# A state-space layer with a gated projection stage on one core: opening rebuilt, last stage's first chunk by pairs

## The reference

```
h   = layernorm(layernorm(x)) * gamma + beta
xz  = h @ W_in.T                          # 512 -> 2048: x_ssm and z, 1024 channels each
xs  = silu(conv4(x_ssm) + conv_b)         # causal, per channel
xp  = xs @ W_xproj.T                      # 33 columns: 1, B (16), C (16)
dt  = softplus(xp @ W_dt.T + b_dt) + 0.001
A   = -exp(A_log)                         # 1024 x 16
h_t = clip(dA*h + (1-dA)/(A+1e-8)*B_t*xs_t, -10, 10),  dA = exp(A*dt_t)
y_t = sum_n C_t[n]*h_t[n] + D*xs_t
x   = x + (y * silu(z)) @ W_out.T
u   = layernorm(x)
x   = x + u @ W_shared.T + bias + (sum of the two normalized top gate weights) * (u @ W_expert.T)
```

## Time and profile before

| | us |
|---|---|
| Median of three runs | 4454.98 (4453.03 to 4458.05) |
| Profiled execution | 4454.84 |
| Its span | 4453.1 |
| PE busy | 4166.3 (94%) |
| DVE busy | 3676.1 (83%) |
| ACT busy | 3171.4 (71%) |
| POOL busy | 3138.2 (70%) |

### The profile page before, as it was taken

The page is one execution under the profiler, slowest core; times in us unless marked ns, Lnnn a source line. Parts: engine busy times, 40 slices in busy tenths (PEclk is TensorE's granted clock), DMA queues, the critical chain, the costliest instruction groups (busy, mean ns, idle before and its releaser), DMA issues. The chain is left out here.

```text
span 4453.1 us, 48998 instructions
## 1 busy us (share of the span) xinstructions
PE 4166.3 (94%) x14186; PEld 2461.5 (55%) x14186; DVE 3676.1 (83%) x4321; ACT 3171.4 (71%) x5821; POOL 3138.2 (70%) x1550
## 2 busy tenths in 40 slices
PE   2999999995999999999999999999999759999999
PEld 1777777774444444444444444444444238888887
DVE  5888888884899999999999999999999744444443
ACT  1666666664899999999999999999999611211111
POOL 0111111110899999999999999999999767777772
PEclk9999999997999999999999999999999879999999
DMA  5566566666576576656665766576656445555550
GB/s 187 190 203 207 186 208 212 214 205 196 152 191 189 155 184 185 184 155 186 187 181 156 193 186 172 158 197 188 168 168 181 142 157 162 169 163 175 176 166 30
DMA packets 581176, 786.71 MB, mean 177 GB/s; under 512 B 102800, under 2 KB 305936, under 8 KB 579368
## 3 DMA queue, kind: packets, MB, share of 16 engines
q1 hardware_dynamic: 570344, 762.57, 58.4%
q10 hardware_dynamic: 10560, 20.97, 1.3%
HBM read 540.17 MB, written 245.18 MB: 176 GB/s over the span
## 5 line engine op out<-in xcount | busy, mean ns | idle before, releaser
L965 POOL TENSOR_TENSOR q<-g,cc 128x1024 f32<-128x1024 f32 x1024 | 2394.6, 2371 | 139.7 <-DVE g L1105 120.6
L1105 DVE TENSOR_TENSOR_SCAN g<-dd,carry,ps_a 128x512 f32<-128x512 f32 x2048 | 2400.3, 1253 | 40.2 <-ACT ps_a L987 24.5
L1045 PE MATMUL ps_y<-q,w_s 128*128 128x512 f32 x4096 | 2098.4, 593 | 24.4 <-POOL q L965 12.7
L987 ACT ACTIVATE ps_a<-dt_s,small 128x512 f32<-128x512 f32 x2048 | 1501.7, 733 | 5.4 <-DVE g L1105 5.4
L976 ACT ACTIVATE dd<-ps_d 128x512 f32<-128x512 f32 x2048 | 1287.7, 629 | 74.7 <-PE ps_d L1032 51.7
L1032 PE MATMUL ps_d<-dm,xk 99*128 99x512 f32 x2048 | 1119.1, 547 | 63.7 <-ACT dd L976 25.9
L1032 PEld LDWEIGHTS ps_d<-dm,xk 99*128 99x128 f32 x2048 | 384.0, 188 | 1223.0 <-ACT dd L976 957.7
L1045 PEld LDWEIGHTS ps_y<-q,w_s 128*128 128x128 f32 x4096 | 778.6, 191 | 184.7 <-issue 59.3
L353 POOL TENSOR_TENSOR xnt_lo<-xnt_f,xnt_hi 128x512 fp32r<-128x512 f32 x64 | 112.5, 1758 | 557.1 <-ACT xnt_hi L378 557.1
L499 PE MATMUL ps_r_f<-xnt_hi,w_hi 128*128 128x512 f32 x1024 | 418.5, 409 | 13.8 <-DVE w_lo L672 13.8
L499 PE MATMUL ps_r_f<-xnt_lo,w_hi 128*128 128x512 f32 x1024 | 402.9, 393 | 0.0
(11 more groups left out here) (162 smaller groups left out, 4439.5 us busy)
## 6 DMA issues: line engine op xcount, KB each, us to landing
w_s<-w_d SPq DMA_DIRECT2D x256, 512.0 KB, 3.8
xk<-xt_d SPq DMA_DIRECT2D x768, 132.0 KB
xt_d<-xt_f SPq DMA_DIRECT2D x256, 256.0 KB, 3.1
cc<-c_d SPq DMA_DIRECT2D x128, 512.0 KB, 11.3
dm<-band_d SPq DMA_DIRECT2D x192, 264.0 KB
xs_d<-xs_f SPq DMA_DIRECT2D x128, 256.0 KB, 2.5
zs_d<-zs_f SPq DMA_DIRECT2D x128, 256.0 KB, 3.0
dt_d<-lg_f SPq DMA_DIRECT2D x32, 1024.0 KB, 6.5
```

The costliest lines, as they stand in the source:

```text
L965: pool.tensor_tensor(q[:, s % QB:s % QB + 2, :], g[:, s % GB:s % GB + 2, :], rows, ALU.mult).then_inc(s_q, 2)
L987: act.activation(ps_a[:, s % AB, :], dt[:, blk % DTB, :], ACT.Exp, scale=small[:, blk % MD, S_A + n:S_A + n + 1]).then_inc(s_a, 1)
L1045: pe.matmul(ps_y[:, blk % 2, :], w[:, half % WB, at:at + P], q[:, s % QB, :], start=(n == 0), stop=(n == NS - 1)).then_inc(s_n, 1)
L1105: dve.tensor_tensor_scan(g[:, s % GB, :], dd[:, m % 2, n, :], ps_a[:, s % AB, :], carry[:, m, n:n + 1], ALU.add, ALU.mult).then_inc(s_g, 1)
```

## The change

- `setup` is gone. Its POOL memsets and DVE steps move into `front`'s streams; the DVE steps stand behind the lowering of the weights, in smaller tiles that share room with the convolution buffers. `small` stays in SBUF for both stages, without D.
- W_in comes in four transfers of 1 MB (a semaphore each) and is copied and lowered by quarters between the scalings of x. PE's first projection waits for each quarter. x of chunk 1 is loaded before the edges are cleared and before `w_dt` is repaired.
- The diagonals are no longer computed: SP writes zeros to `w_d` (two transfers of 0.5 MB in each of chunks 0 to 7) and then the 2048 diagonal elements of one m (in chunks 1 to 8). The band is cleared in chunks 8 to 11, from a smaller tile of zeros. The transposed inverse goes by way of PE and one DVE copy in chunk 0 to `invt_d`, three times and once as zeros.
- `fill_band(0)` moves to chunk 12 of the front, `gather_ahead` to its end; both must land before the front ends.
- In `ffn` SP issues all loads. Chunk 0 comes by pairs of groups (xs, y and zs of a pair count on one semaphore); some of it waits in `y_lo`, `t_hi`, `t_lo`. Its split runs by pairs, and PE projects the lower half of the channels between the last four row products. The inverse takes four groups of 16 rows, so b and c rows come in two transfers instead of six.

```diff
+                load_x(0)
+                for dst, src in ((a_log, ...), (gamma[:, :], t_in["ln_gamma"]), (beta[:, :], t_in["ln_beta"])):
+                    sp.dma_start(dst, src).then_inc(s_gb, 16)
+                for k in range(KD):
+                    sp.dma_start(raw_win[k], t_in["W_inT"][k * P:(k + 1) * P, :]).then_inc(s_wq[k], 16)
...
+                load_x(1)
+                sp.wait_ge(s_pool, 1)
+                clear_edges()
+                sp.wait_ge(s_lo, KD + 1)
                 sp.dma_start(w_dt[2 * NX:NX3, :].bitcast(F32), low_dt.bitcast(F32)).then_inc(s_wt, 16)
-                load_x(1)
...
+                def clear_diagonal(m, h):
+                    sp.dma_start(w_d[m, :, bass.ts(h, NS * P // 2)].rearrange("p (n k) -> p n k", k=P),
+                                 bcast(zeros[:, 0:1], [(0, NS // 2), (1, P)])).then_inc(s_zero, 16)
+                def fill_diagonal(m):
+                    whole = w_d[m, :, :]
+                    sp.dma_start(bass.AP(tensor=whole.tensor, offset=whole.offset, ap=[(W_PITCH + 1, P), (P, NS)]), inv[:, m, :],
+                                 allow_slow_non_contiguous=True).then_inc(s_diag, 16)
...
                     store_b(ch)
+                    if 0 < ch <= MD:
+                        sp.wait_ge(s_zero, 16 * (EDGES + 2 * ch))
+                        fill_diagonal(ch - 1)
+                    if ch < MD:
+                        clear_diagonal(ch, 0)
+                    elif ch < MD + 4:
+                        clear_band(ch - MD)
+                    elif ch == MD + 4:
+                        sp.wait_ge(s_bto, 32)
+                        sp.wait_ge(s_zero, 16 * (EDGES + 2 * MD + 8))
+                        fill_first_band()
                     store_zs(ch, 6)
                     store_turned(ch, 6)
                     load_x(ch + 2)
                     store_zs(ch, 7)
                     store_turned(ch, 7)
+                    if ch < MD:
+                        clear_diagonal(ch, 1)
...
                 sp.wait_ge(s_xpo, CHUNKS * 32)
+                for b in range(BATCH):
+                    gather_ahead(b)
+                sp.wait_ge(s_diag, 16 * (4 + MD + 2 + BATCH))
...
+                act.wait_ge(s_gb, 48)
+                act.activation(ea, a_log, ACT.Exp).then_inc(s_ea, 1)
+                upper_win(0)
+                scale_xnt(0, 0)
+                scale_xnt(0, 1)
+                upper_win(1)
+                scale_xnt(0, 2)
+                scale_xnt(0, 3)
+                upper_win(2)
+                upper_win(3)
+                act.wait_ge(s_wt, 9 * 16)
                 act.activation(w_dt[:, :], raw_dt, ACT.Copy).then_inc(s_hi, 1)
...
-                fill_band(0)
-                sp.dma_start(small[:, :, :], w_d[:, :, W_BIG:W_COLS].rearrange("m p s -> p m s"), ...)
                 load_x(0, 0)
-                sp.wait_ge(s_band, 32)
                 load_b(0, 0)
...
                 load_c(0, 3)
-                for b in range(BATCH):
-                    gather_ahead(b)
-                sp.wait_ge(s_ba, 16 * BATCH)
                 load_ahead(0)
...
+                load_rows(0)
+                sp.dma_start(raw_inv, invt_d).then_inc(s_wt[0], 16)
                 sp.dma_start(d_par[:, :], t_in["D_param"]).then_inc(s_dp, 16)
-                load_first(0)
-                load_y(0)
+                load_pair(0)
+                load_pair(1)
+                load_weights(1, "W_outT", 0)
+                load_pair(2)
+                load_pair(3)
+                load_weights(2, "W_outT", HALF * P)
                 load_x(0)
+                load_weights(4, "W_expertT", 0)
+                sp.wait_ge(s_hi, 1)
+                sp.wait_ge(s_lo, 1)
+                load_weights(3, "W_sharedT", 0)
...
-                for m in range(MD):
+                pe.wait_ge(s_set, 4)
+                for m in range(HALF):
                     weigh(0, m)
+                for i in range(SUB):
+                    weigh(0, HALF + i)
+                    if i == 0:
+                        pe.wait_ge(s_lo, 2)
+                    project(0, i, 0)
                 pe.wait_ge(s_lo, 3)
                 for i in range(SUB):
-                    project(0, i, 0)
                     project(0, i, 1)
                     weigh(1, 2 * i)
                     weigh(1, 2 * i + 1)
```

More of the change, by code:

```diff
@@ L176, in front @@
-def front(nc, sb, sem, t_in, ident, ones, minus_half, margin, within, clips, xs_d, dt_d, zs_d, xp_d, xt_d, bt_d, c_d):
+            front(nc, sb, sem, t_in, ident, ones, minus_half, margin, within, clips, small, xs_d, dt_d, zs_d, xp_d, xt_d, bt_d, c_d,
+                  band_d, w_d, invt_d, ba_d)
+        scan(nc, sb, sem, clips, small, xs_d, dt_d, xt_d, bt_d, band_d, c_d, w_d, y_d, ba_d)
+        ffn(nc, sb, sem, t_in, ident, minus_half, xs_d, zs_d, xp_d, invt_d, y_d, out)
+def front(nc, sb, sem, t_in, ident, ones, minus_half, margin, within, clips, small, xs_d, dt_d, zs_d, xp_d, xt_d, bt_d, c_d,
+          band_d, w_d, invt_d, ba_d):
@@ L217, in front @@
         S = lambda n: sem("f_" + n, c)
-        s_wt, s_x, s_one, s_hi, s_lo, s_b1 = S("weights"), S("x"), S("one"), S("hi"), S("lo"), S("b1")
+        s_wt, s_x, s_one, s_hi, s_lo = S("weights"), S("x"), S("one"), S("hi"), S("lo")
+        s_wq = [S(f"wq{k}") for k in range(KD)]
+        s_gb, s_pool, s_ea, s_set = S("gb"), S("pool"), S("ea"), S("set")
+        s_ivm, s_ivt, s_zero, s_diag = S("ivm"), S("ivt"), S("zero"), S("diag")
         s_st, s_pow, s_xn, s_tr, s_te, s_xl = S("stats"), S("pow"), S("xn"), S("tr"), S("te"), S("xl")
@@ L229, in front, with plain @@
         raw_dt = xs[0:NX3, 0:2, :].rearrange("p m t -> p (m t)")
+        raw_win = [t[:, h * XHALF:(h + 1) * XHALF, :].rearrange("p m t -> p (m t)") for t in (v, lg) for h in range(2)]
+        a_log, ea, ap_, an = (conv[:, 1, bass.ts(i, MD * NS)].rearrange("p (m n) -> p m n", n=NS) for i in range(4))
+        raw_invt = v[0:NS, 0:2, :].rearrange("p m t -> p (m t)")
         low_dt = xt[0:NX, 0, 0:2, :].rearrange("p s t -> p (s t)")
+        def plain(ch, q):
+            return conv[:, 0, :] if ch == 0 and q % 2 else xnt[:, :]
         def made(ch, kind, m):
@@ L310, in _ @@
                     store_xs(ch, 3)
+                    if ch == 0:
+                        sp.wait_ge(s_ivt, 1)
+                        for r in range(3):
+                            sp.dma_start(invt_d[NS * r:NS * (r + 1), :, :].rearrange("n m p -> n (m p)"), raw_invt).then_inc(s_diag, 16)
+                        sp.dma_start(invt_d[3 * NS:4 * NS, :, :], bcast(zeros[0:NS, 0:1], [(0, MD), (1, P)])).then_inc(s_diag, 16)
                     store_zs(ch, 0)
@@ L742, in _, with scan @@
                 dve.wait_ge(s_fl, 3)
-def scan(nc, sb, sem, ident, clips, xs_d, dt_d, xp_d, xt_d, bt_d, band_d, c_d, w_d, y_d, ba_d):
+def scan(nc, sb, sem, clips, small, xs_d, dt_d, xt_d, bt_d, band_d, c_d, w_d, y_d, ba_d):
     STEPS = MD * NS
@@ L778, in scan @@
         S = lambda n: sem("s_" + n, c)
-        s_sm, s_band, s_ba = S("small"), S("band"), S("ba")
+        s_band, s_ba = S("band"), S("ba")
         s_dm = [S(f"dm{i}") for i in range(PIECES)]
@@ L1360, in upper_weights, with upper_first @@
                     act.activation(parts[i][1], parts[i][0], ACT.Copy).then_inc(s_hi, 1)
-                def upper_inverse():
-                    act.wait_ge(s_wt[0], 96)
-                    for h in range(2):
-                        last = act.activation(inv[:, h::2, :], raw_inv[h], ACT.Copy)
-                    last.then_inc(s_hi, 1)
+                def upper_first(j):
+                    act.wait_ge(s_mul, 2 * j + 2)
+                    act.activation(y_hi[:, 2 * j:2 * j + 2, :], y[:, 2 * j:2 * j + 2, :], ACT.Copy).then_inc(s_yh, 1)
                 def upper_y(ch):
```

362 lines of the change are left out of this document (159 added, 203 removed).

## The result

| | before | after |
|---|---|---|
| Median (6 runs each) | 4453.09 us (4451.33 to 4458.05) | 4472.84 us (4455.33 to 4474.16) |
| Ratio, 95% interval | | 1.0033 (1.0023 to 1.0043) |
| Profiled execution, span | 4454.84, 4453.1 us | 4471.99, 4470.2 us |
| Granted clock over the span | 0.981 | 0.976 |

Slower, by 0.3% (0.2 to 0.4; the medians alone differ by 0.44%); the forecast was 4360 us, 2% faster than before. Five of the six runs of after lie between 4471.2 and 4474.2, one at 4455.33; that one has no trace, so it stays unexplained.

A forecast was written before the change was run, and what follows sets the result against it. It took PE to bound front chunks and POOL's products to pace the scan, with gains only where they wait. -64.6 + 8 - 2.2 + 3 - 11 - 28 = -94.8 on 4453.1 gave 4358.3, predicted 4360 us; 4343 to 4375 at 0.65.

The forecast's parts named there:

- A: Opening: without `setup`, x loads first and weights come by quarters; gain 64.6 us, bounds 60 and 66.
- B: Front chunks: added zero and diagonal transfers on SP delay the load of x; loss 8 us, bounds 0 and 16.
- slack of 2.2 us: Front chunk: what DVE can lose to late x, 1.1 after the statistics and 1.1 at the turned tile.
- sign of being wrong: Front chunks: the prediction is wrong if a chunk period, expected at 59.7 us, grows by over 2.
- The forecast of 8: Front chunks: loss taken from an overflow of 13.6 us, less because chunks where x has margin give less.
- x is late by more than costed: Rival, front: SP's issues of thousands of descriptors also hold up stores; loss 20 to 40 us, chance 0.13.
- C: Into the scan: dropped band fill and `small` load gain 2.2 us; the gather at front's end loses 3, bounds 0 and 7.
- D: Early scan: with no gather there, `cc` loads leave earlier and POOL waits less; gain 11 us, bounds 8 and 12.3.
- E: Into the last stage: rows and y load ahead of weights, so mixing starts earlier; gain 28 us, bounds 18 and 33.

The follow-up runs named there:

- all_behind: The changed kernel with every clear of diagonals and bands and every fill moved out of the front's chunk loop, behind it: 4534.61 us, ratio 1.0166 to before.
- combined: The changed kernel with the x load ahead of fills and clears, and 32 unused bytes ahead of `dt` in the scan: 4362.78 us, ratio 0.9788 to before.
- before_off32: The kernel before with 32 unused bytes ahead of `dt` in the scan, nothing else changed: 4510.31 us, ratio 1.0114 to before.

## Why the prediction was wrong

**A held** (64.8 for 64.6), with the marks that it named: first projection 21.71, `xz` 31.67.

**B failed, on its prices.** The step and the place were right: it put the x load behind these transfers, saw a slack of 2.2 us, and said that DVE's wait would grow and PE would wait at `xp`'s transposition. It priced a diagonal 1.0, a clear 1.4 and a band part 2.8; by themselves they took 2.7, 3.9 and 6.2 (all_behind). Its prices came from the tiny packets of the old opening (8.1 ns) and from 1 us of mixed loads (21.8 ns); zeros and elements going to HBM took 61 and 21 ns of an engine. It put x 2.4 us later, and x landed 6.0 later. With the measured prices its own formula gives: 2.7 + 3.9 + 0.8 - 2.2 = 5.2 in seven chunks, 2.7 + 6.2 + 0.8 - 2.2 = 7.5 in one, 4.8 in three, 58 in all; measured 57.4. That the two agree so closely is in part luck: the formula leaves out the clear of chunk 0 (2.5 more) and has no term for PE's longer busy time, which is 22 of the 57.4. The prediction's own sign of being wrong, a chunk period grown by over 2, came true in 12 of the 15 periods. The forecast of 8 also took off for margin where there was none, and its upper bound of 16 was little more than the same prices without that, no bound on the prices. The prediction set beside its price the 10.5 ns a packet of the Trainium skill (DMA: Bandwidth & Descriptors, "Measured") and made a diagonal 1.3 of it. The page gets this figure, for loads issued from GpSimd, from 0.67 us for the 64 packets of one whole transfer, so it may not be divided by 16 engines again. Undivided, as an estimate, it makes a diagonal 21.5 us. The trace agrees with neither: 2.7. The rival "x is late by more than costed" was the right mechanism, priced 20 to 40.

**C** cost 2.7 instead of 0.8: from the issue of the dt store (1067.01 before, 1059.72 after) to the first `xk` load it is 9.56 before (to 1076.57) and 12.27 after.

```profile
1059.72 2.57 SPq L186 DMA_DIRECT2D dt_d<-lg_f  x2
1062.34 2.16 SPq L243 DMA_DIRECT2D ba_d<-xp_d  x2
...
1071.99 1.20 SPq L839 DMA_DIRECT2D xk<-xt_d  x3
```

With the 2.2 of the dropped issues, the gather costs 4.9, between the bounds 0 and 7 and nearer to the upper one. That is the side on which the Trainium skill's rule on completions to HBM (DMA: Bandwidth & Descriptors, "Anatomy of one DMA") had put it; the 4.9 isn't split into issue and completion.

**D held where it can be seen.** The first 128 `g` of the scan took 165.2 us before and 153.5 in combined, 11.7 less (forecast 11). POOL's wait for `cc`, 14.2, fell to 5.1 there and to 4.6 in after, a little over the 4 that was named. In after the stalls of placement cover half of the gain (159.5).

**The missing term.** The prediction said "the change leaves its steady part alone" and costed the scan's other 15 chunks at nothing: +50.7 us (153.59 - 150.21, 15 times). This is the largest miss of the forecast; B's, 57.4 for 8, is nearly as large. The instructions are the same, but the diff moved `small` and cut it by 32 bytes, and no step asked what stands behind it; before_off32 shows that 32 bytes alone do it. This alone turned a gain of some 34 us into a loss of 17. No trace of before could have priced it; that the allocation moves could have been read from the diff.

**E nearly held.** From the start of the last matmuls of the scan (3528.95 before, 3570.14 after) the first self-term came after 17.1 instead of 27.9, 10.8 nearer (14 named), the last residual of chunk 0 after 78.4 instead of 102.6, 24.3 nearer (28 named). The timelines of DVE, POOL and PE, answering to the earlier trace rows:

```profile
3587.27 0.75 DVE L1610 SCALAR_TENSOR_TENSOR xs_c<-ps_b,d_par_c,xs_c 128x512 f32<-128x512 f32 x1 [2.16 <-PE ps_b L1466]
...
3592.76 2.42 POOL L1360 TENSOR_TENSOR y_lo<-y_c,y_hi 128x1024 fp32r<-128x1024 f32 x1 [6.53 <-ACT y_hi L1398]
...
3602.39 0.76 PE L1456 MATMUL ps_c<-wo_hi,y_hi 128*128 128x512 f32 x1 [5.15 <-POOL y_lo L1360]
...
3648.51 0.69 DVE L1588 TENSOR_TENSOR x_c<-ps_c,x_c 128x512 f32<-128x512 f32 x1 [2.04 <-PE ps_c L1456]
```

What was late is the start: PE waits 14.24 us for the rows that POOL makes (its row products begin at 3586.37), which the forecast did not cost. Behind it the projections took 6.8 us each ((3648.51 - 3628.02)/3); the forecast had 6.3, though 9.3 less 12 products of 0.22 is 6.7.

With x first and the 32 bytes put back, the forecast comes out: combined has a span of 4353.9, where the prediction had 4358.3. It doesn't bear out B's price, since x no longer waits for these transfers; its loop lost 3.7. D came out some 2 better than forecast there, and E some 2 worse.

## What to carry over

- Ahead of a load that someone waits for, price every transfer by its rate when the queue holds nothing else, and bound the price, not only the slack: here three prices were short by a factor of 2.2 to 2.8. Ask when the consumer is ready: x was free to land until 22.7 us after the `xp` copy, and cost time from there on. Then ask whether the order is needed at all: one moved line was worth 54 us.
- A tile that is added, dropped or resized moves all tiles behind it. Keep tiles that DMAs fill in short rows (here 512 bytes) on multiples of 256 bytes, and list their addresses before and after an edit, also in stages that the edit doesn't touch.
- Where a stage with unchanged instructions slows down, compare the mean time of its DMA packets by size first.

## What the hardware showed

- A 512-byte row from HBM into SBUF took 30.8 to 31.0 ns of a DMA engine with the tile on a multiple of 256 bytes, 33 on one of 128, 34.1 on one of 64, and 35.0 to 35.7 on one of 32; packets of 4096 bytes stayed between 234.6 and 242.0. This was worth 2% of a scan in which the DMA engines were busy 66% of the time, and 91 and 93% in the stretch shown.
- Zeros written from SBUF to HBM in 512-byte pieces, read from one element again and again, ran at 133 GB/s, where the mix of loads at the earlier trace rows had 387. Which of the three, piece, source or direction, sets this, no run shows. Single elements ran at 1.3 ns each over all engines (15,761 packets in 21 us).
- In the front's loop of after, five of six gaps of 1.8 to 2.0 us in PE were followed by 3.4 us of clock at 1.2 GHz (from 2.4); in the scan stretches of 3.4 or 6.8 us at 1.2 GHz stood with gaps of 1.9 to 5.1 us, mostly waits for `xk`. Over the front's loop PE's idle time grew by 36 us (40.6 for 5.1), and its busy time for the same instructions by another 22 (917.1 for 895.2), of which the lower clock is 8.5.
